# Attention over a 768-channel image: the key maximum taken by GpSimd in place of TensorE and VectorE

## What is computed

```python
qkv = x_flat @ W_qkv.T                       # 12 heads of 64
var_v = jnp.var(v, axis=-1, ddof=1, keepdims=True)
var_k = jnp.var(k, axis=-1, ddof=1, keepdims=True)
scores = var_v @ jnp.swapaxes(var_k, -2, -1) * scale
attn = jax.nn.softmax(scores, axis=-1)
out = attn @ v                               # then out @ W_proj.T + b_proj
x = x + _L0_conv_ref(_gn(x), ...)            # _gn: group norm, 32 groups
```

## Time and profile before

| | us |
|---|---|
| median of 3 runs | 2156.47 |
| lowest, highest | 2149.06, 2156.99 |
| the profiled execution, its time | 2150.42 |
| its span in the trace | 2148.6 |
| mean granted TensorE clock in it | 0.976 |

### The profile page before, as it was taken

How to read it: one execution, slowest core, us unless ns; L and a number is a source line. 1 busy time by engine, 2 the same in 40 slices (tenths; PEclk the granted TensorE clock), 3 DMA queues, 4 the chain that set the end, 5 groups by cost and what they waited for, 6 DMA issues and landing times.

```text
span 2148.6 us, 33881 instructions
## 1 busy us (share of the span) xinstructions
PE 2012.0 (94%) x13100; PEld 1110.7 (52%) x13100; DVE 1701.1 (79%) x3695; ACT 1181.1 (55%) x1285; POOL 182.2 (8%) x215
## 2 busy tenths in 40 slices
PE   3899999999999999999999999999999999999970
PEld 2656347662565536554375535655365543755330
DVE  7587566998689875998769986798769987699748
ACT  5466733766267643677336762566436773367601
POOL 2000000110001000111001100011001110011001
PEclk8999999999999999999999999999999999999985
DMA  6411302335033431335113350233313351133304
GB/s 230 161 51 61 99 1 80 111 117 157 2 100 129 137 99 37 113 107 180 31 51 129 121 166 1 90 129 124 123 35 115 104 183 30 46 124 129 109 1 176
DMA packets 102977, 214.36 MB, mean 100 GB/s; under 512 B 50080, under 2 KB 50848, under 8 KB 102816
## 3 DMA queue, kind: packets, MB, share of 16 engines
q1 hardware_dynamic: 70848, 95.79, 15.0%
q0 software_dynamic: 25920, 94.38, 11.9%
q10 hardware_dynamic: 6048, 22.02, 3.2%
HBM read 154.08 MB, written 57.74 MB: 99 GB/s over the span
## 4 chain that ended last, share of the span: by engine, by line
PE 67%; DVE 13%; DMA 9%; ACT 5%; issue 3%; SPq 1%; POOL 1%; ACTq 0%; DVEq 0%; POOLq 0%
PE ps L1122 26%; PE ps L1162 22%; PE ps L1179 14%; ACT ring L606 4%; PE ps L1144 3%; DMA a_sb<-a_rows 2%; DVE bt L813 2%; DVE bst_x L736 2%; DVE st L762 1%; DMA cs_rows_y<-mv_y 1%; DMA dt_sb<-d_sb 1%; DMA bt<-r_rows 1%; DVE d_sb L823 1%; DVE xv L882 1%; DVE xv L880 1%
## 5 line engine op out<-in xcount | busy, mean ns | idle before, releaser
L606 ACT ACTIVATE ring<-a_sb,coef 128x1024 f32<-128x1024 f32 x768 | 813.4, 1137 | 19.6 <-PE ps L1162 9.6
L1122 PE MATMUL ps<-wkv_hi,h_sp 128*128 128x256 f16 x4608 | 778.3, 274 | 14.1 <-DVE h_sp L753 10.2
L1162 PE MATMUL ps<-ring,xv 128*64 128x512 f32 x3072 | 689.6, 597 | 0.6 <-ACT ring L606 0.6
L1122 PE MATMUL ps<-wkv_lo,h_sp 128*128 128x256 f16 x2304 | 630.4, 274 | 0.0
L1122 PEld LDWEIGHTS ps<-wkv_hi,h_sp 128*128 128x128 f16 x4608 | 452.2, 98 | 101.9 <-issue 31.0
L813 DVE TENSOR_TENSOR bt<-bt,ring 128x1024 f32<-128x1024 f32 x416 | 485.2, 1214 | 2.2 <-ACT ring L606 1.8
L1162 PEld LDWEIGHTS ps<-ring,xv 128*64 128x64 f32 x3072 | 208.1, 137 | 406.8 <-issue 390.1
L590 ACT ACTIVATE xv<-ps 128x256 f32<-128x256 f32 x192 | 72.5, 382 | 594.1 <-DVE st L762 594.1
L1179 PE MATMUL ps<-xv,wp_hi 128*128 128x512 f16 x1152 | 354.1, 385 | 0.7 <-DVE xv L973 0.6
L762 DVE BATCH_NORM_STATS2 st<-ps 128x6 f32<-128x64 f32 x1536 | 218.7, 213 | 121.2 <-PE ps L1122 121.1
L1122 PEld LDWEIGHTS ps<-wkv_lo,h_sp 128*128 128x128 f16 x2304 | 226.1, 98 | 26.6
(11 more groups left out here) (127 smaller groups left out, 1322.0 us busy)
## 6 DMA issues: line engine op xcount, KB each, us to landing
a_sb<-a_rows SPq DMA_DIRECT2D x96, 512.0 KB, 4.8
xv<-in_x POOLq DMA_DIRECT2D x48, 512.0 KB, 3.7
h_sp<-in_x ACTq DMA_DIRECT2D x42, 512.0 KB, 4.5
shift_rows<-bt POOLq DMA_DIRECT2D x42, 512.0 KB, 3.0
out<-xv POOLq DMA_DIRECT2D x42, 512.0 KB, 2.9
bt<-r_rows SPq DMA_DIRECT2D x80, 256.0 KB, 3.9
shift_rows<-ring SPq DMA_DIRECT2D x12, 528.0 KB, 14.5
xv<-in_L_conv_W_qkv SPq DMA_DIRECT2D x4, 1152.0 KB, 9.4
```

What stands on the lines that cost most here:

```text
L606: nc.scalar.activation(ring_of(p, s, m), a_sb[:, h % 4, :], ACT.Exp, scale=coef[:, h, m:m + 1]).then_inc(s_exp, 1)
L1122: last = nc.tensor.matmul(ps[:, kv_bank[u % 2], half * 2 * P:(half + 1) * 2 * P], h_sp[:, k, hp, m * P:(m + 1) * P], wkv[wpart][:, k, q * ...
L1162: last = nc.tensor.matmul(ps[s * HD:(s + 1) * HD, o_bank[p % 2] + j, :], v_sb[:, p, m, s * HD:(s + 1) * HD], ring_of(p, s, m)[:, j * HALF: ...
```

## The change

The second transpose, the two small VectorE steps and the spread go. GpSimd takes the maximum over the 128 partitions of `kmx` with one `partition_all_reduce`, which leaves it in all partitions of a new tile `kall` in SBUF. In GpSimd's list it stands at the head of each turn of `layer1` (pair t of the next image at tile t), and six times in the start for the first image. VectorE's `k_max` becomes `a_out` with the copy alone, at the same places; `k_scales` stays where it is and waits for `s_kall`.

```diff
+            def k_reduce(b, q):
+
+                pool.wait_ge(s_kmx, b * NP + q + 1)
+                nc.gpsimd.partition_all_reduce(kall[:, :], kmx[:, :], P, ABSMAX).then_inc(s_kall, 1)
+
             def layer1(b):
                 for t in range(CT + 1):
                     if t < CT:
+                        k_reduce(b + 1, t)
                         pool.wait_ge(s_gn, b * CT + t + 1)
...
                     pool.dma_start(x1[:, t, :], x_t[0, :, t, :]).then_inc(s_x1in[t], 16)
+                for q in range(NP):
+                    k_reduce(0, q)
                 group_pow(pool, "x", 1)
...
-            def k_max(b, q, later):
+            def a_out(b, q, later):
 
                 dve.wait_ge(s_ktp, b * NP + q + 1)
                 if later or q:
                     dve.wait_ge(s_arow, (b * NP + q) * 16)
-                nc.vector.tensor_reduce(kmx1[:, :], ps_kt, AX_X, ALU.max).then_inc(s_kch, 1)
                 nc.vector.tensor_copy(at[:, :], ps_at).then_inc(s_at, 1)
-                dve.wait_ge(s_kch, b * NP + q + 1)
-                nc.vector.tensor_scalar(kdiag[:, :], ident[0:2, 0:2], kmx1[:, 0:1], None, ALU.mult).then_inc(s_kdiag, 1)
 
             def k_scales(b, q):
 
-                dve.wait_ge(s_kmp, b * NP + q + 1)
+                dve.wait_ge(s_kall, b * NP + q + 1)
                 nc.vector.tensor_tensor(coef[:, 2 * q:2 * q + 2, :], m2[:, 2:4, :],
-                                        ps_km.unsqueeze(2).broadcast_to((P, 2, MT)), ALU.subtract).then_inc(s_cch, 1)
+                                        kall[:, :].unsqueeze(2).broadcast_to((P, 2, MT)), ALU.subtract).then_inc(s_cch, 1)
...
-            def k_transpose(b, q):
+            def a_transpose(b, q):
 
                 pe.wait_ge(s_kmx, b * NP + q + 1)
-                nc.tensor.transpose(ps_at, av[:, :, :].rearrange("p s m -> p (s m)"), ident[:, :])
-                nc.tensor.transpose(ps_kt, kmx[:, :], ident[:, :]).then_inc(s_ktp, 1)
-
-            def k_spread(b, q):
-                pe.wait_ge(s_kdiag, b * NP + q + 1)
-                nc.tensor.matmul(ps_km, ones[0:2, :], kdiag[:, :], start=True, stop=True).then_inc(s_kmp, 1)
+                nc.tensor.transpose(ps_at, av[:, :, :].rearrange("p s m -> p (s m)"), ident[:, :]).then_inc(s_ktp, 1)
```

More of the change, by code:

```diff
@@ L166, in gn_attention_displace @@
         kmx = sb("kmx", [P, 2])
-        kmx1 = sb("kmx1", [2, 1])
-        kdiag = sb("kdiag", [2, 2])
+        kall = sb("kall", [P, 2])
         coef = sb("coef", [P, NH, MT])
@@ L186, in gn_attention_displace @@
         ps_at = ps[0:2 * MT, 7, 0:P]
-        ps_kt = ps[0:2, 7, P:2 * P]
-        ps_km = ps[:, 7, 2 * P:2 * P + 2]
         s_wkv_in = [sem(f"s_wkv_in{n}") for n in range(4)]
@@ L231, in gn_attention_displace @@
         s_at = sem("s_at")
-        s_kch = sem("s_kch")
-        s_kdiag = sem("s_kdiag")
-        s_kmp = sem("s_kmp")
+        s_kall = sem("s_kall")
         s_cch = sem("s_cch")
@@ L899, in phase_a @@
                         variances(b, 0)
-                        k_max(b, 0, l1 is not None)
+                        a_out(b, 0, l1 is not None)
                         if l1 is not None:
@@ L925, in span @@
                             if p == 4:
-                                k_max(b, p + 1, later)
+                                a_out(b, p + 1, later)
                             if later:
@@ L1188, in phase_a @@
                         kv_unit(b, u, later, (0,))
-                        k_transpose(b, 0)
+                        a_transpose(b, 0)
                         kv_unit(b, u, later, (1,))
-                        k_spread(b, 0)
                     else:
@@ L1203, in span @@
                             kv_unit(b, nxt + m // 2 + 1, later)
-                        if m == 4 and p <= 3:
-                            k_spread(b, p + 1)
                         weigh(b, p, m, later)
                         if p <= 4 and m == (3 if p <= 3 else 1):
-                            k_transpose(b, p + 1)
-                        if m == 3 and p == 4:
-                            k_spread(b, p + 1)
+                            a_transpose(b, p + 1)
                         if p == NP - 1 and m in (3, 5):
```

## The result

The changed kernel takes 2128.73 us (median of 4 runs, 2127.27 to 2135.85) against 2156.73 for the kernel before; ratio 0.9883, 95% interval 0.9851 to 0.9916. It is 28 us faster by the medians, where the sum said 25.4 and the forecast 2129.

What follows compares the result with a forecast made beforehand. TensorE's list was taken as the bound in `span` and `phase_a`. Its five terms sum to 25.4 us: 2125.0 from the profiled 2150.4, 2131.1 from the median 2156.5; forecast 2129 between them, range 2119 to 2142.

Steps and rivals of the forecast that it cites:

- Terms 1 to 5: TensorE: second transpose 5.3 us, spreads at pair 0 2.8, pair 1 6.1, pairs 2 to 4 7.5, pair 5 3.7.
- term 2: Spread of pair 0, between two units: removal gives 0.40 us in each of seven later images, 2.8 us.
- Term 3: Spread of pair 1 in the seven later images: removal gives 0.87 us each, 6.1 us.
- The cost of nothing: GpSimd's added reduction and its waits: a 0.4 us reduction fits everywhere, so no time is added.
- Rival A: At pairs 0 and 1 exponentials and additions set the pace: only 16.5 us gained, about 2134 us; 12%.
- Rival B: GpSimd's change of kind is long: TensorE stands from about T = 17, gain eaten at T = 18.7; slower, 6%.
- T: Time GpSimd needs to prepare when its kind of operation changes: between 0 and 10.1 us, cost taken as nothing.
- both rooms: Room for T on GpSimd: 10.6 us behind y's power, 16.4 us ahead of x's power.
- the formula: Loss at GpSimd's kind changes: 13 x (T - 16.7), equal to the 25.4 us gain at T = 18.7.
- Rival C: VectorE keeps GpSimd out, stretching the reductions 2.2 times to 0.9 us or holding them: no change, about 2150 us; 6%.
- Rival D: TensorE gains the gross gaps (0.51, 1.08), ordinary step not subtracted: 10 us more, 2115 us; 2%.

Runs made afterwards that it cites:

- e2: The changed kernel with the second transpose of kmx kept on TensorE, read by nobody; 2133.07 us, ratio 0.9908.
- e3: The changed kernel with the small matmul of the spread kept on TensorE at its old places, of a constant tile, read by nobody; 2140.45 us, ratio 0.9938.
- e4: The kernel before, whole, with GpSimd's reduction beside it and VectorE waiting for it, result unused; 2154.76 us, ratio 1.0005.
- e1: The changed kernel again, no edit; 2130.07 us against 2154.44 for the kernel before, ratio 0.9886.
- e9: The changed kernel once more, no edit; 2132.01 us, ratio 0.9888 to the kernel before.
- e7: The changed kernel with a small GpSimd multiplication of another kind ahead of the reduction at all 48 pairs; 2132.32 us, ratio 0.9908.
- e8: The changed kernel with the reduction of pair 0 repeated 28 times in the seven later images; 2187.07 us, ratio 1.0180.
- e12: The changed kernel with the reduction of pair 0 repeated 14 times in the seven later images; 2131.94 us, ratio 0.9906.
- e11: e10 with the first adding of the projection put between the two parts of the x statistics on VectorE; 2121.45 us, ratio 0.9846.
- e5: The changed kernel with an image's last reciprocal ahead of the statistics of next x tiles 0 to 3 on VectorE; 2131.3 us, ratio 0.9911.
- e10: e5 with the last normalisation of an image moved ahead of the statistics of next x tiles 2 to 5; 2138.85 us, ratio 0.9931.

## Why the prediction was right, and what it missed

- *What bounds it.* Right: TensorE's list. e2 and e3, which give the removed entries back to TensorE with nobody reading them, give back the time by stage, 0.11 us for each transpose and 0.64 and 1.39 us for the spreads of an image at pair 0 and at pairs 1 to 5.
- *Terms 1 to 5.* Each stage within 0.02 us where no new wait came: 0.98 at pair 0, 1.82 at pairs 1 to 5; term 2 is confirmed by e3's rows (0.40). Term 3, the largest for one place, counted on the exponentials being there; they were. The period of an image was put down as some 3.4 us shorter; the terms themselves give 3.3.
- *GpSimd.* The cost of nothing is shown by e4. The reduction is 0.36 us beside an idle VectorE and 1.24 to 1.29 beside a busy one, three times as long where I had allowed 2.2; at the tightest place, pair 0, 2.9 us of room remain. The order of GpSimd's list held.
- *Rival A,* that part does not come back: wrong at its place (pairs 0 and 1), but right in kind at another. Of the 1.8 us missing at pairs 1 to 5, 1.2 are seen at pair 5, in three images. In one of them ScalarE waits for the broadcast row, and TensorE, 8 us later, for ScalarE:

```profile
998.56 1.15 ACT L609 ACTIVATE ring<-a_sb,coef 128x1024 f32<-128x1024 f32 x1 [0.68 <-DMA a_sb<-a_rows]
```

```profile
1006.48 1.94 PE L1157 MATMUL ps<-ring,xv 128*64 128x512 f32 x8 [0.43 <-ACT ring L609]
```

  And behind the last pair VectorE is later with respect to TensorE than before: 2.5 us more of waiting for the reciprocal. The step that the prediction lacks is this one: it had no term for the projection, neither for the waits there nor for the time at 1.2 GHz.
- *The number.* The three profiled spans of the changed kernel are 14.6, 9.7 and 18.6 us shorter than that of before, 7 to 16 us short of the sum; in the timed runs it won 28.0, 24.4 and 22.5, about the sum. In part this is the choice of profiles: that of before is 6 us faster than its median, and those of changed and e1 are the slowest of their groups, with more time at 1.2 GHz in the projection than e9's. How much of the rest is loss and how much spread stays open. So the agreement of 2128.73 with 2129 to a fraction of a microsecond is partly luck: the forecast was placed by judgement between 2125.0 and 2131.1, and the runs of the changed kernel spread over 9 to 17 us.
- *Rival B,* the change of kind: T is about 6 us (up to 8.3 in e7), below both rooms; behind the start the changed kernel has 15 changes between the reduction and the power, not 13, and none costs. The point from which it decides was set too late: the room behind y's power is 10.6 us and then 4.4 to 4.6 more, so by e8 and e12 TensorE stands from a T of about 15, not 17, and each of e8's seven stands came with 6.8 us at 1.2 GHz, some 2.5 us of loss that the formula lacked.
- *Rival C:* the stretching is there, up to 1.29 us in the changed kernel and 2.72 in e7; the cost is not (e4, e7).
- *Rival D:* wrong; the ordinary step of 0.20 us stays.

## What to carry to other kernels

Where one engine's list sets the pace, cost an edit from start to start on that engine, ordinary step subtracted, and check that the new supplier's answer comes inside the gap to its reader; that sum was right to 0.02 us for each stage of an image in which no new wait came. Before handing an engine a second kind of work, find the idle time at each change of kind: 6 us a change were free here because 7.5 and some 16 us of idle time lay there. And when a list shrinks, look at the next place where it waits for another engine's order: in the three profiles of the changed kernel it waits 1.9 to 3.4 us more there than before, and three moves in VectorE's list (e11) took 10.6 us off the changed kernel. Split such a stretch into waits and time at 1.2 GHz before laying its length to the change: three profiles of the same changed kernel have 23.9 to 30.7 us of the second.

## What the runs showed of the hardware

- GpSimd's reduction over the partitions of a 128 x 2 tile takes 0.36 to 0.41 us beside an idle VectorE or small operations, and 1.24 to 1.29 when VectorE begins a 128 x 1024 or 128 x 992 operation with two inputs 0.2 us ahead of it. It then ends 0.2 us behind VectorE's operation: at every pair 1 (1.24 to 1.26 us beside line 813) and every pair 2 to 4 of the later images (1.28 to 1.29 beside line 867), never at pair 5, where VectorE runs nothing beside it. In e7 it lasts up to 2.72 us beside three such operations in a row. Small tiles on GpSimd were priced here by what VectorE ran beside them.
- Changing from a two-input operation to this reduction costs GpSimd 5.7 to 6.9 us with no record, and 7.3 to 8.3 at seven of eight pairs 5 (e7). The time passes while GpSimd waits: in the changed kernel the reduction of pair 0 starts 0.14 us after its input, 7.5 us behind the power. A DMA instruction follows the reduction without delay (0.15 us behind it in e8).
- TensorE's clock fell to 1.2 GHz for 3.4 or 6.8 us behind most of its stands ahead of the spread of the reciprocals (changed kernel: 6.8 us behind stands of 2.8, 2.5 and 2.8 us, 3.4 us behind stands of 1.5 and 1.0, none behind one of 0.9), but not behind e5's two stands of 1.5 and 0.3 to 1.1 us in each image. In e10 seven stands of 2.7 to 3.2 us brought four falls, and none came with three of 2.8, 3.0 and 3.1 us. In e8 the clock fell for 6.8 us at each of seven stands of 6.1 us, 0.9 to 3.2 us before the stand was over. Which stands bring a fall was not settled; what it costs is half of its length (the constant rest in the table of the projection).
